# Activation rows stored with their statistics, and a reordered attention and second routing, in a two-layer Macaron block

## The chip, the cores and the metric

The kernel runs on one core of a Trainium2 chip. The metric is the device time of one execution in microseconds (us). The profile gives the span of one profiled execution, which is a little shorter than that execution's own time.

## The reference

Input x has 2 batches of 2048 tokens of width 128. Three layers follow one another: half a feed-forward, an attention, half a feed-forward.

```python
x = x + 0.5 * ffn(layernorm(x))
x = x + attn(layernorm(x))
x = x + 0.5 * ffn(layernorm(x))

# ffn: 4 experts, 128 -> 512 -> 128, each token keeps the one of its largest gate logit
idx = argmax(softmax(x @ Wg + bg))
y = gelu(x @ W1[e] + b1[e]) @ W2[e] + b2[e];  out = y[e == idx]

# attn: linear attention with 32 features
q_prime = elu((x @ Wq.T) @ proj) + 1;  k_prime = elu((x @ Wk.T) @ proj) + 1
kv = k_prime.T @ (x @ Wv.T)
out = (q_prime @ kv) / (sum(q_prime) + 1e-8)
```

Everything is float32.

## The kernel before

**Phases and visits.** A feed-forward of one batch is a phase. `ph` 0 and 1 are the first layer of batches 0 and 1, `ph` 2 and 3 the last layer. The tokens of a batch are sorted by expert into 16 tiles of 128 rows. A phase walks the tiles in 19 visits (16 tiles and 3 for tiles that two experts share). Visit `v` of phase `ph` has the running number `s = 19*ph + v`; there are 76. For a visit TensorE does `up` (line 966: 8 matmuls from `hT_in` and `slab` into `U`) three visits ahead and `down` (line 977: 8 matmuls into `DN`); ScalarE does the gelu between (`hT`, line 1145), VectorE adds the result to the row in `finish` (line 729) and the bias of b2 in `residual` (line 717). In visits 4 to 11 of phases 1 and 2 (`full`) a matmul adds the bias instead. `down(s)` waits for `finish(s-2)`.

**Rows.** The rows lie in HBM as `rows0` and `rows1`, 144 numbers each: 128 activations and 16 columns with mean, reciprocal deviation and token number. GpSimd fetches one sorted tile with an indirect DMA (`gather`, line 430), with a memset of `rest` (line 416) ahead of most of them. VectorE normalises a tile (`norm`, xn, line 705) at the visit that the tables `NORM_*` name; TensorE transposes it (`turn_in`, line 957) in groups, of which tiles 6 and 7 form one that is turned at visit 2. SyncE (SP in the profile) copies the weights of each visit into a `slab`, five visits ahead, and stores the rows: `store_x` (line 306) the activations, `store_stats` (line 287) the 16 columns, each in two halves for each batch, and `store_rows1` after the attention.

**Routing.** `route_hot`, `route_slots`, `route_hots`, `visit_tables` and `route_src` on VectorE, `counts` and `inverse` on TensorE, `place_tiles` on GpSimd and `hots` on ScalarE make the sorted order of the next phase. They lie at visits counted from `hot_at`: HOT0 in phase 0, HOT1 in phases 1 and 2. `route_slots` ends in the tile matrix `A1` (line 651); `route_src` gives the indices `src` (line 691), for which the next gathers wait. `FIRST1 = HOT1 + 4` is the visit at which GpSimd begins to gather the last layer's tiles.

**Attention.** In phase 0 and 1 VectorE takes statistics of finished rows in four groups of tiles; GpSimd raises each to the power -0.5 (`pow_la`, RS, line 401); TensorE projects each group (`side_turn`, `side_kq`) and VectorE scales it (`la_scaled`: lines 750 to 752, LGX, KQ, KM). The last group and all else of the attention of batch 0 lies in visits 0 to 6 of phase 1, that of batch 1 in visits 0 to 6 of phase 2: `la_exp` (ScalarE, which loads another table for it and back), `la_features` (KQ, KR), `la_z`, the sums `la_sum` on TensorE, `la_fold`, `la_gt`, `la_kv`, and four times `lb_num` (TensorE) and `lb_x2` (VectorE), with a power on GpSimd after each (`pow_lb`, line 406). Then `route_hot` follows.

**GpSimd's stream** is written by hand. In phase 1 from visit FIRST1 on it gathers tiles of batch 0 for phase 2 (`gather_first`: one tile and two tiles by turns), and between them runs `pow_la` of batch 1 at visits 10, 12, 15 and 18. In phase 2 it scatters finished tiles of batch 0 to the output (line 442), gathers batch 1's last tiles two at a time, and then scatters all that remain: those of batch 0 from tile `DONE0` on, and 16 of batch 1. Until the pair with tile PAIRS1 of batch 1 every second scatter goes without a `rest` ahead of it, after it all.

**Start.** TensorE fills the time until the first tile with matmuls on `mean_w` (`busy`, line 898); the last such stretch is `busy(24)`, after the gates and the visit tables, and `turn_in` of tile 0 follows it.

## Time and profile before

| | us |
|---|---|
| Three runs | 236.08, 238.13, 237.55 |
| Median | 237.55 |
| The profiled execution, its own time | 237.53 |
| Its span | 235.8 |
| TensorE matmuls busy | 207.2 (88%) |
| VectorE busy | 159.4 (68%) |
| GpSimd busy | 160.2 (68%) |
| ScalarE busy | 126.9 (54%) |

1.73 us of the profiled execution lie outside its span. The busy shares are averages over stages with different limits. PE, DVE, ACT, POOL and SP stand for TensorE, VectorE, ScalarE, GpSimd and SyncE in the rows. In a timeline row the first number is the start in us from the span's start, the second the length in us.

### The profile page before, as it was taken

How to read it: one execution, taken by the hardware profiler on the slowest of the kernel's cores; microseconds unless marked ns; L12 is line 12 of the kernel's file. 1: busy time of each engine (PE TensorE's matmuls, PEld its weight loads, DVE VectorE, ACT ScalarE, POOL GpSimd, SP SyncE). 2: the span in 40 equal slices, each digit the busy share in tenths (PEclk: the TensorE clock that was granted, in tenths of full speed). 3: DMA queues.
4: the chain of work that ended last, by engine and by line, in shares of the span. 5: the costliest groups of instructions: out<-in, count | busy, mean ns of one | idle time of the engine just before them, and what ended most of it. 6: DMA issues, size and time to landing. Idle time of an engine off the chain costs nothing. (4 is left out here: it accounts for less than half of the span.)

```text
span 235.8 us, 6375 instructions
## 1 busy us (share of the span) xinstructions
PE 207.2 (88%) x1786; PEld 195.7 (83%) x1786; DVE 159.4 (68%) x641; ACT 126.9 (54%) x406; POOL 160.2 (68%) x225
## 2 busy tenths in 40 slices
PE   8989996996997999999969998999959899999900
PEld 7879996896997988889969897779959899999900
DVE  3699463579688989698887879788776545553400
ACT  1415055567554586635675676825565567765500
POOL 7221888882728687147138888756878888788775
PEclk9999999998899999999999999999979999999985
DMA  4999259982534462326703852517721976662111
GB/s 103 372 321 254 96 199 351 314 212 83 185 110 167 154 215 69 130 106 237 277 0 116 300 206 83 165 61 281 269 79 42 329 274 222 222 221 103 45 56 45
DMA packets 28454, 41.69 MB, mean 177 GB/s; under 512 B 7795, under 2 KB 14851, under 8 KB 28422
## 3 DMA queue, kind: packets, MB, share of 16 engines
q1 hardware_dynamic: 22368, 34.11, 40.5%
q0 software_dynamic: 3072, 6.82, 11.1%
q10 hardware_dynamic: 2982, 0.36, 1.0%
q8 instruction: 16, 0.26, 0.5%
q14 instruction: 16, 0.13, 0.2%
HBM read 9.41 MB, written 6.82 MB: 69 GB/s over the span
## 5 line engine op out<-in xcount | busy, mean ns | idle before, releaser
L1145 ACT ACTIVATE hT<-U,slab 128x128 f32<-128x128 f32 x304 | 86.7, 370 | 56.4 <-PE U L966 56.3
L966 PE MATMUL U<-hT_in,slab 128*128 (+1 forms) x608 | 82.8, 280 | 1.5 <-ACT hT_in L1139 1.3
L977 PE MATMUL DN<-W,hT 128*128 (+1 forms) x608 | 83.7, 282 | 0.2 <-issue 0.2
L966 PEld LDWEIGHTS U<-hT_in,slab 128*128 128x128 f32 x608 | 74.8, 194 | 2.7 <-issue 2.4
L977 PEld LDWEIGHTS DN<-W,hT 128*128 128x128 f32 x608 | 75.4, 195 | 1.4 <-issue 1.2
L430 POOL DMA_INDIRECT G<-rows,src x64 | 62.5, 977 | 15.2 <-issue 10.2
L729 DVE SCALAR_TENSOR_TENSOR G<-DN,mask,G 128x128 f32 (+1 forms) x76 | 26.4, 348 | 27.3 <-PE DN L977 24.6
L416 POOL MEMSET rest<- 128x512 f32 (+1 forms) x78 | 35.4, 454 | 6.3 <-DVE G L729 0.7
L442 POOL DMA_INDIRECT out_dram<-G x32 | 31.6, 988 | 7.3 <-issue 6.3
L705 DVE TENSOR_SCALAR xn<-G 128x128 f32<-128x128 f32 x64 | 23.7, 389 | 9.3 <-DMA G<-rows,src 9.0
L717 DVE SCALAR_TENSOR_TENSOR G<-slab,mask,G 128x128 f32 (+1 forms) x60 | 21.2, 353 | 6.7 <-DVE G L729 4.0
L1139 ACT ACTIVATE hT_in<-TR 128x128 f32<-128x128 f32 (+1 forms) x44 | 14.4, 327 | 17.8 <-PE TR L957 17.4
L957 PE MATMUL TR<-ident,xn 128*128 128x128 f32 x64 | 14.6, 280 | 7.5 <-DVE xn L705 6.3
L401 POOL TENSOR_TENSOR RS<-VE,neghalf 128x4 f32<-128x4 f32 x8 | 8.5, 1062 | 12.9 <-DVE VE L741 12.8
L406 POOL TENSOR_TENSOR G<-VE,neghalf 128x4 f32<-128x4 f32 x8 | 8.3, 1043 | 12.8 <-DVE VE L799 12.6
L957 PEld LDWEIGHTS TR<-ident,xn 128*128 128x128 f32 x64 | 8.3, 142 | 8.8 <-DVE xn L705 7.2
L898 PE MATMUL DN<-mean_w 128*128 128x128 f32 x104 | 14.6, 300 | 1.1 <-POOL mean_w L362 1.1
L898 PEld LDWEIGHTS DN<-mean_w 128*128 128x128 f32 x104 | 13.9, 215 | 1.1 <-POOL mean_w L362 1.1
L467 POOL TENSOR_TENSOR AV<-A,lane_f 128x256 bf16<-128x256 bf16 x4 | 3.3, 828 | 12.5 <-DVE A L651 6.9
L396 POOL TENSOR_TENSOR MR<-VE,neghalf 128x8 f32<-128x8 f32 x4 | 6.7, 1679 | 5.7 <-DVE VE L564 5.2
L734 DVE BATCH_NORM_STATS2 ST<-G 128x6 f32<-128x128 f32 x32 | 8.8, 287 | 1.6 <-issue 1.4
L656 DVE TENSOR_TENSOR SL<-slot_i,lane_b 128x512 bf16<-128x512 int32 x12 | 8.8, 784 | 0.0
(159 smaller groups left out, 219.7 us busy)
## 6 DMA issues: line engine op xcount, KB each, us to landing
slab<-W SPq DMA_DIRECT2D x76, 322.0 KB, 3.1
rows<-G SPq DMA_DIRECT2D x8, 288.0 KB, 2.1
rows<-X SPq DMA_DIRECT2D x4, 512.0 KB, 9.5
X<-in_L_attn_x_dram SPq DMA_DIRECT2D x4, 256.0 KB, 6.7
X<-in_L_attn_x_dram SPq DMA_DIRECT2D x2, 512.0 KB, 8.8
W<-in_L_ffn_W_dram SPq DMA_DIRECT2D x1, 1024.0 KB, 11.5
W<-in_L_ffn_W_dram SPq DMA_DIRECT2D x4, 256.0 KB, 6.0
G<-rows,src POOLq DMA_INDIRECT x64, 3.2
```

Of the source, the lines that this page charges most:

```text
L416: eng.memset(rest[:, 0:columns], 0.0)
L430: eng.indirect_dma_start(out=row(f, b, t, 0, RW), out_offset=None, in_=(rows0, rows1)[f][b], in_offset=bass.IndirectOffsetOnAxis(ap=src[f] ...
L442: eng.indirect_dma_start(out=out_rows, out_offset=bass.IndirectOffsetOnAxis(ap=index, axis=0), in_=row(1, b, t), in_offset=None, engine_se ...
L705: ffn["norm"].done(eng.tensor_scalar(xn[k % NXN][:, :], row(f, b, t), row(f, b, t, D, 1), row(f, b, t, D + 1, 1), ALU.subtract, ALU.mult))
L717: ffn["res"].done(eng.scalar_tensor_tensor(out=r, in0=slab[s % NSLAB][:, F + NC:SW], scalar=mask[f][b][:, v:v + 1], in1=r, op0=ALU.mult, o ...
L729: ffn["out"].done(eng.scalar_tensor_tensor(out=r, in0=DN[s % 2][:, 0:D], scalar=mask[f][b][:, v:v + 1], in1=r, op0=ALU.mult, op1=ALU.add))
L898: eng.matmul(DN[0][:, 0:P], mean_w[:, :], mean_w[:, :], start=True, stop=True)
L957: last = eng.transpose(TR[:, i * P:(i + 1) * P], xn[k % NXN][:, :], ident[:, :])
L966: i = eng.matmul(U[s % 3][:, c * P:(c + 1) * P], slab[s % NSLAB][:, c * P:(c + 1) * P], hT_in[ph % 2][:, bass.ds(v * P - expert_at[s], P)] ...
L977: i = eng.matmul(DN[s % 2][:, 0:D], hT[s % NHT][:, c * P:(c + 1) * P], W2[:, bass.ds(expert_at[s] + c * NE * D, D)], start=(c == 0 and not ...
L1139: ffn["xTs"].done(eng.activation(hT_in[ph % 2][:, first * P:(first + n) * P], TR[:, 0:n * P], ACT.Copy))
L1145: i = eng.activation(hT[s % NHT][:, c * P:(c + 1) * P], U[s % 3][:, c * P:(c + 1) * P], ACT.Gelu, bias=slab[s % NSLAB][:, F + c:F + c + 1])
```

## The change

**Rows.** Activations and statistics of a batch share one tile `XR` of 144 columns. For batch 1 the load writes straight into it; for batch 0 ScalarE copies the activations over (`copy_rows`, four instructions after the fourth `front_copy`). A half batch is then stored by one DMA of 1152 contiguous numbers for each partition. For batch 0 these two stores stand on SP behind the four loads of W2; for batch 1 at visits 5 and 6 instead of four stores at visits 2, 4, 7 and 8.

**Order of phases 1 and 2, visits 0 to 9.** Each step of the attention comes up to one visit earlier and HOT1 goes from 7 to 6, and with it FIRST1 from 11 to 10. Two instructions of `route_slots` (`end_i`, `flo_i`) move to `visit_tables`.

```diff
@@ -111,9 +111,12 @@
-        X0 = several("X0_", [P, T, D], B)
...
+        XR = several("XR", [P, T, RW], B)
+        X0 = [sb("X0", [P, T, D])[:, :, :], XR[1][:, :, 0:D]]
         ST0 = several("ST0_", [P, T, 6], B)
-        MR0 = several("MR0_", [P, T, RW - D], B)
+        MR0 = [r[:, :, D:RW] for r in XR]
         VE0 = several("VE0_", [P, T], B)
@@ -207,8 +211,8 @@
         NORM_LATE = (-5, -4, -3, -2, -1, 0, 1, 1, 2, 3, 4, 5, 6, 7, 8, 9)
-        NORM_MID = (-5, -4, -3, -2, -1, 0, 0, 1, 1, 2, 2, 3, 4, 5, 7, 8)
-        NORM_EARLY = (-5, -4, -3, -2, -1, 0, 0, 1, 1, 2, 2, 3, 4, 5, 6, 6)
+        NORM_MID = (-5, -4, -3, -2, -1, 0, 0, 0, 3, 3, 4, 4, 5, 5, 7, 8)
+        NORM_EARLY = (-5, -4, -3, -2, -1, 0, 0, 0, 3, 3, 4, 4, 5, 5, 6, 6)
@@ -268,7 +272,7 @@
         UP_LEAD, RES_LEAD, SLAB_LEAD = 3, 2, 5
-        HOT0, HOT1 = 5, 7
+        HOT0, HOT1 = 5, 6
         FIRST0, FIRST1 = HOT0 + 4, HOT1 + 4
@@ -280,11 +284,6 @@
-        def store_stats(eng, b, h):
-            lo, hi = h * T // 2, (h + 1) * T // 2
-            need(eng, ln0["rstd"], 2 * b + h)
-            eng.dma_start(rows0_v[b][:, lo:hi, D:RW], MR0[b][:, lo:hi, :]).then_inc(s_rows0[b], 16)
@@ -300,10 +299,14 @@
-            def store_x(b, h):
-                for i in range(h * XN[b] // 2, (h + 1) * XN[b] // 2):
-                    eng.wait_ge(s_x[b][i], 16)
-                eng.dma_start(rows0_v[b][:, h * H:(h + 1) * H, 0:D], X0[b][:, h * H:(h + 1) * H, :]).then_inc(s_rows0[b], 16)
+            def store_rows0(b, h):
+                need(eng, ln0["rstd"], 2 * b + h)
+                if b == 0:
+                    eng.wait_ge(s_copied, (h + 1) * XN[0] // 2)
+                else:
+                    eng.wait_ge(s_x[b][h], 16)
+                eng.dma_start(rows0_v[b][:, h * H:(h + 1) * H, :].rearrange("p t c -> p (t c)"),
+                              XR[b][:, h * H:(h + 1) * H, :].rearrange("p t c -> p (t c)")).then_inc(s_rows0[b], 16)
@@ -311,10 +314,10 @@
             eng.dma_start(w1_v[:, :, F + NC:SW], b2.unsqueeze(0).to_broadcast([P, NE, D])).then_inc(s_w["b2"], 16)
-            store_x(0, 0)
-            store_x(0, 1)
             for e in range(NE):
                 load_w2(e)
+            store_rows0(0, 0)
+            store_rows0(0, 1)
@@ -349,10 +352,8 @@
                     copy_slab(s + SLAB_LEAD)
-                if ph == 0 and v in (2, 4):
-                    store_x(1, v // 2 - 1)
-                if ph == 0 and v in (7, 8):
-                    store_stats(eng, 1, v - 7)
+                if ph == 0 and v in (5, 6):
+                    store_rows0(1, v - 5)
                 if ph in (1, 2) and 6 <= v < 6 + NG:
@@ -452,12 +453,10 @@
                     pow_la(ph, NG - 1)
-                if ph > 0 and v == 4:
-                    pow_lb(o, 0)
-                if ph == 2 and v == 4:
-                    scatter(0, 0)
-                if ph > 0 and 4 <= v < 3 + NG:
-                    pow_lb(o, v - 3)
+                if ph > 0 and v in (4, 5, 6):
+                    pow_lb(o, v - 4)
+                if ph > 0 and v == 6:
+                    pow_lb(o, 3)
                 if ph < B and v in VAR_AT[ph]:
@@ -476,8 +475,8 @@
-            SCATTERS = {5: (1,), 6: (2,), 7: (3,), 8: (4,), 9: (5,), 10: (6,)}
-            DONE0, PAIRS1 = 7, 10
+            SCATTERS = {v: (v - 4,) for v in range(4, FIRST1)}
+            DONE0, PAIRS1 = FIRST1 - 4, 10
@@ -520,7 +519,7 @@
                     place_tiles(3)
-                if v >= FIRST1:
+                if FIRST1 <= v < FIRST1 + T // 2:
                     gather(1, 1, 2 * (v - FIRST1), columns=2 * P)
@@ -639,10 +638,8 @@
                 need(eng, rt["cb"], ph)
-                did(eng.tensor_tensor(wh3[:, :, :], wh[:, :, :], hot[:, :, :], ALU.mult), False)
-                did(eng.tensor_copy(end_i[:, :], c3[:, 0:NE - 1, T - 1]))
-                did(eng.tensor_reduce(pos[:, :], te(wh3), AX.X, ALU.add), False)
-                did(eng.tensor_scalar(flo_i[:, :], end_i[:, :], 7, None, ALU.arith_shift_right))
+                did(eng.tensor_tensor(wh3[:, :, :], wh[:, :, :], hot[:, :, :], ALU.mult))
+                did(eng.tensor_reduce(pos[:, :], te(wh3), AX.X, ALU.add))
                 did(eng.tensor_copy(pos_i[:, :], pos[:, :]))
@@ -659,6 +656,9 @@
                 e_no = exp_no[:, 1:NE, 0]
+                ends = cum[:, :].rearrange("p (e t) -> p e t", e=NE)[:, 0:NE - 1, T - 1]
+                did(eng.tensor_copy(end_i[:, :], ends))
+                did(eng.tensor_scalar(flo_i[:, :], end_i[:, :], 7, None, ALU.arith_shift_right))
                 did(eng.scalar_tensor_tensor(out=vis[:, :], in0=flo_i[:, :], scalar=float(T - 1), in1=e_no, op0=ALU.min,
@@ -832,22 +832,21 @@
                 f, b = divmod(ph, 2)
+                o = ph - 1
+                if ph in (1, 2) and v == 3:
+                    la_kv(o)
                 finish(s)
                 if ph in (1, 2):
-                    o = ph - 1
                     if v == 1:
-                        la_scaled(o, NG - 1)
+                        la_features(o, 2, NG)
+                        la_z(o, 0, NG)
                     if v == 2:
-                        la_features(o, NG - 1, NG)
-                        la_z(o, NG - 1, NG)
-                    if v == 3:
                         la_gt(o)
-                        la_kv(o)
                     if v == 4:
-                        lb_x2(o, 0)
                         lb_x2(o, 1)
-                    if v in (5, 6):
-                        lb_x2(o, v - 3)
+                    if v == 5:
+                        lb_x2(o, 2)
+                        lb_x2(o, 3)
                 r = (0, 1) if ph == 0 else (1, ph - 1)
@@ -858,6 +857,8 @@
                     norm(*ahead)
+                if ph in (1, 2) and v == 0:
+                    la_scaled(o, NG - 1)
                 if ph == 0 and v == hot_at + 2:
@@ -878,9 +879,9 @@
                     if v == 0:
-                        la_features(o, 0, NG - 1)
-                    if v == 1:
-                        la_z(o, 0, NG - 1)
+                        la_features(o, 0, 2)
+                    if v == 3:
+                        lb_x2(o, 0)
                 if ph < B + 1:
@@ -1016,7 +1017,7 @@
             def la_q(b):
-                need(eng, la["z"], 2 * b + 1)
+                need(eng, la["z"], b)
                 for g in range(NG):
@@ -1072,22 +1073,27 @@
                 ph, v = divmod(s, V)
+                hot_at = HOT0 if ph == 0 else HOT1
+                o = ph - 1
+                if ph in (1, 2) and v == 0:
+                    side_turn(o, NG - 1)
                 down(s)
+                if ph in (1, 2):
+                    if v == 3:
+                        la_kv(o)
+                        la_q(o)
+                    if v == 4:
+                        lb_num(o, 1)
+                    if v == 5:
+                        lb_num(o, 3)
                 for ahead in groups_of(ph, v):
                     turn_in(*ahead)
-                hot_at = HOT0 if ph == 0 else HOT1
                 if ph in (1, 2):
-                    o = ph - 1
                     if v == 0:
-                        side_turn(o, NG - 1)
-                    if v == 1:
                         side_kq(o, NG - 1)
-                    if v == 3:
-                        la_q(o)
-                        la_fold(o)
-                    if v in (4, 5, 6):
-                        lb_num(o, (0, 2, 3)[v - 4])
-                if ph == 0 and v == hot_at + 2:
+                    if v == 2:
+                        la_sum(o, 2, 4)
+                if ph < B + 1 and v == hot_at + 2:
                     counts(ph + 1)
@@ -1103,14 +1109,10 @@
                     if v == 2:
-                        la_sum(o, 2, 4)
-                    if v == 3:
-                        la_kv(o)
-                    if v == 4:
-                        lb_num(o, 1)
-                    if v == hot_at + 2:
-                        counts(ph + 1)
-                    if v == hot_at + (3 if ph == 2 else 4):
+                        la_fold(o)
+                    if v in (3, 4):
+                        lb_num(o, 2 * (v - 3))
+                    if v == hot_at + 4:
                         inverse(ph + 1, 0, NG)
@@ -1133,6 +1135,11 @@
+            def copy_rows(i):
+                lo, hi = i * T // XN[0], (i + 1) * T // XN[0]
+                eng.wait_ge(s_x[0][i], 16)
+                eng.activation(XR[0][:, lo:hi, 0:D], X0[0][:, lo:hi, :], ACT.Copy).then_inc(s_copied, 1)
@@ -1187,10 +1194,10 @@
                 front_copy(k)
+            for i in range(XN[0]):
+                copy_rows(i)
             front_copy(NG)
             front_copy(NG + 1)
-            store_stats(eng, 0, 0)
-            store_stats(eng, 0, 1)
             hots(0, NG - 1)
@@ -1207,16 +1214,16 @@
                 late = ph in (1, 2) and v in (0, 1, 2)
-                if late and v == 1:
-                    la_exp(ph - 1, 3, 4)
-                if late and v > 0:
-                    gelu(s + UP_LEAD - 1)
                 if ph in (1, 2):
...
                         side_copy(o * NG + NG - 1)
+                        la_exp(o, 0, NG)
                     if v == 2:
                         la_part(o)
+                if late and v > 0:
+                    gelu(s + UP_LEAD - 1)
+                if ph in (1, 2):
                     if v == 3:
@@ -1228,8 +1235,6 @@
                         hots(ph + 1, g)
-                if ph < B and v == 18:
-                    la_exp(ph, 0, 3)
```

Two hunks are left out: the new semaphore `s_copied`, and the wait for 32 instead of 64 counts of `s_rows0` ahead of the first gather of a phase.

On SyncE, the program's first DMAs (X, XR: activations; W: W1, then W2 at the line of `load_w2`; rows_0: the HBM rows of batch 0). Before:

```order
L298 DMA X_0<-in_L_attn_x_dram 128x512 x4
L298 DMA X_1<-in_L_attn_x_dram 128x1024 x2
L312 DMA W<-in_L_ffn_W_dram 128x4x512
L313 DMA W<-in_L_ffn_b_dram 128x4x128
L306 DMA rows_0<-X_0 128x8x128 x2
L301 DMA W<-in_L_ffn_W_dram 128x4x128 x4
```

After:

```order
L297 DMA X<-in_L_attn_x_dram 128x512 x4
L297 DMA XR<-in_L_attn_x_dram 128x8x128 x2
L315 DMA W<-in_L_ffn_W_dram 128x4x512
L316 DMA W<-in_L_ffn_b_dram 128x4x128
L300 DMA W<-in_L_ffn_W_dram 128x4x128 x4
L308 DMA rows_0<-XR 128x1152 x2
```

The stores of rows_0 have gone behind W2's loads, and each moves 1152 numbers in a row for each partition.

On GpSimd, from the third `pow_la` of batch 1 (RS1_1) to the fourth, in phase 1 (visits 15 to 18); G1_0 is the last layer's rows of batch 0. Before:

```order
L401 TENSOR_TENSOR RS1_1<-VE1_1,neghalf 128x4
L416 MEMSET rest 128x512
L430 DMA G1_0<-rows1_0,src1_0 128x144
L416 MEMSET rest 128x512
L430 DMA G1_0<-rows1_0,src1_0 128x144
L416 MEMSET rest 128x512
L430 DMA G1_0<-rows1_0,src1_0 128x144
L416 MEMSET rest 128x512
L430 DMA G1_0<-rows1_0,src1_0 128x144
L401 TENSOR_TENSOR RS1_1<-VE1_1,neghalf 128x4
```

After:

```order
L402 TENSOR_TENSOR RS1_1<-VE1_1,neghalf 128x4
L417 MEMSET rest 128x512
L431 DMA G1_0<-rows1_0,src1_0 128x144
L417 MEMSET rest 128x512
L431 DMA G1_0<-rows1_0,src1_0 128x144
L417 MEMSET rest 128x512
L431 DMA G1_0<-rows1_0,src1_0 128x144
L417 MEMSET rest 128x512
L431 DMA G1_0<-rows1_0,src1_0 128x144
L417 MEMSET rest 128x512
L431 DMA G1_0<-rows1_0,src1_0 128x144
L402 TENSOR_TENSOR RS1_1<-VE1_1,neghalf 128x4
```

Four gathers stood between the third and the fourth RS1_1, now five. Between the second and the third it was three and is four; ahead of the second stand three in both.

On VectorE, visits 0 and 1 of phase 2 (KQ1, LGX1, KM1: group 3 of the attention of batch 1; L729 is `finish`, L705 `norm`, L717 `residual`). Before:

```order
L729 SCALAR_TENSOR_TENSOR G1_0<-DN1,mask1_0,G1_0 128x128
L750 COPY LGX1<-S0 128x16
L751 TENSOR_TENSOR KQ1<-S0,RS1_1 128x4x2x32
L752 TENSOR_SCALAR KM1<-KQ1 128x2x128
L705 TENSOR_SCALAR xn7<-G1_0 128x128
L705 TENSOR_SCALAR xn0<-G1_0 128x128
```

After:

```order
L729 SCALAR_TENSOR_TENSOR G1_0<-DN0,mask1_0,G1_0 128x128
L705 TENSOR_SCALAR xn5<-G1_0 128x128
L705 TENSOR_SCALAR xn6<-G1_0 128x128
L705 TENSOR_SCALAR xn7<-G1_0 128x128
L750 COPY LGX1<-S0 128x16
L751 TENSOR_TENSOR KQ1<-S0,RS1_1 128x4x2x32
L752 TENSOR_SCALAR KM1<-KQ1 128x2x128
L717 ISA
L717 SCALAR_TENSOR_TENSOR G1_0<-slab5,mask1_0,G1_0 128x128
L758 SCALAR_TENSOR_TENSOR KQ1<-KQ1,KM1 128x2x128
```

`la_scaled` of the last group stood behind the `finish` of visit 1; now it stands in visit 0, ahead of the `residual` and of all `la_features`.

## Rows read from the trace of the kernel before

**Rows 1.** The chain of work that ended last, its end: start, length, what

```profile
223.57 0.36 DVE G L729
...
225.62 0.96 POOL out_dram L442
...
233.20 0.95 POOL out_dram L442
```

**Rows 2.** Timeline of GpSimd, phases 2 and 3: start, length, what, idle before

```profile
171.56 0.61 POOL L467 TENSOR_TENSOR AV<-A,lane_f 128x256 bf16<-128x256 bf16 x1 [0.60 <-DVE A L651]
...
176.79 0.99 POOL L430 DMA_INDIRECT G<-rows,src  x1 [0.43 <-issue]
...
199.15 0.95 POOL L430 DMA_INDIRECT G<-rows,src  x1 [0.15 <-issue]
...
203.45 0.96 POOL L442 DMA_INDIRECT out_dram<-G  x1 [0.16 <-issue]
...
206.21 0.97 POOL L442 DMA_INDIRECT out_dram<-G  x1 [0.16 <-issue]
```

**Rows 3.** Timeline of all engines, the start of the program

```profile
23.25 5.55 PE L898 MATMUL DN<-mean_w 128*128 128x128 f32 x48
24.10 1.20 POOL L430 DMA_INDIRECT G<-rows,src  x1 [4.30 <-DMA rows<-MR]
...
35.76 0.60 SPq L306 DMA_DIRECT2D rows<-X  x1
...
36.35 0.95 POOL L430 DMA_INDIRECT G<-rows,src  x1 [0.15 <-issue]
...
41.04 0.42 DVE L705 TENSOR_SCALAR xn<-G 128x128 f32<-128x128 f32 x1 [2.48 <-DMA G<-rows,src]
...
41.51 0.44 PE L957 MATMUL TR<-ident,xn 128*128 128x128 f32 x2 [2.25 <-DVE xn L705]
```

**Rows 4.** Busy time in stretches of 2 us; then granted clock, DMA share, GB/s

```profile
8.00:10.00 2.00, 2.00 (x20) 2.00 (x20) 1.90 (x14) 0.79 (x2) 0.26 (x1) 1.00 1.05 407
...
18.00:20.00 2.00, 2.00 (x20) 2.00 (x20) 1.97 (x6) 1.54 (x5) 1.00 (x1) 1.00 1.28 263
```

**Rows 5.** Timeline of GpSimd, phase 1 from visit 10 on

```profile
121.55 1.01 POOL L401 TENSOR_TENSOR RS<-VE,neghalf 128x4 f32<-128x4 f32 x1 [3.39 <-DVE VE L741]
...
123.20 1.04 POOL L430 DMA_INDIRECT G<-rows,src  x1 [0.17 <-issue]
...
127.80 1.05 POOL L401 TENSOR_TENSOR RS<-VE,neghalf 128x4 f32<-128x4 f32 x1
...
139.30 0.96 POOL L430 DMA_INDIRECT G<-rows,src  x1 [0.15 <-issue]
...
141.08 0.96 POOL L430 DMA_INDIRECT G<-rows,src  x1 [0.16 <-issue]
142.06 1.18 POOL L401 TENSOR_TENSOR RS<-VE,neghalf 128x4 f32<-128x4 f32 x1
```

**Rows 6.** Timeline of TensorE, visits 0 and 1 of phase 2

```profile
138.49 1.06 PE L977 MATMUL DN<-W,hT 128*128 x8
...
142.88 1.13 PE L998 MATMUL S<-Wkq,xTs 128*128 128x96 f32 x8
```

**Rows 7.** Timeline of VectorE, phase 2, attention and routing

```profile
144.04 0.17 DVE L750 COPY LGX<-S 128x16 f32<-128x16 f32 x1
...
171.06 0.42 DVE L651 TENSOR_TENSOR A<-tile_i,lane_f 128x256 bf16<-128x256 int32 x1
...
174.85 0.17 DVE L691 TENSOR_SCALAR src<-tok 128x16 int32<-128x16 f32 x1
```

**Rows 8.** Timeline of TensorE around the second routing of phase 2

```profile
172.87 0.25 PE L940 MATMUL S<-AV,SL 128*128 128x32 bf16 x4 [2.22 <-DVE SL L656]
...
174.32 2.07 PE L977 MATMUL DN<-W,hT 128*128 x8
```

**Rows 9.** Busy time in a stretch of 2 us, as in Rows 4

```profile
174.00:176.00 2.00, 2.00 (x17) 1.99 (x18) 1.08 (x5) 1.24 (x5) 1.70 (x3) 0.50 0.09 33
```

3 lines of the change are left out of this document (2 added, 1 removed).

## Prediction

> **What bounds the kernel now.** I read the chain of work that ended last first. The last `finish` ends at 223.93, yet GpSimd goes on scattering until 234.15, one scatter every 1.26 us (225.62 to 233.20 are seven of them) [rows 1]. Those scatters' data were ready before; GpSimd is behind. So the next view is its timeline, to find where it last waited for something [rows 2]. From the first of the last sixteen gathers at 176.79 it is never idle for more than 0.3 us: fifteen steps to 199.15 are 1.49 us each, then come 25 scatters, two in 2.76 us with a `rest` ahead of every second one (203.45 to 206.21). The end is therefore fixed by the start at 176.79, and TensorE's end at 223 has 10 us to spare. That start hangs on the routing: `A1` is done at 171.48, `place_tiles` comes at 171.56, two scatters follow, then the gather [rows 2, 7]. `src`, its other condition, is done at 175.02 [rows 7].
>
> Ahead of that, each step waits in turn for VectorE's chain of attention and routing (phases 1 and 2), and at the start there is one large hole in TensorE: 2.25 us ahead of 41.51, for a tile whose gather was issued at 36.35 and was there only at 41.04 [rows 3].
>
> All times below are on the clock of the trace of before. Its execution took 237.53 us, 0.02 from the median, so a difference in the span is taken as one of the median.
>
> **Start.** The first gather waits for the statistics' stores until 24.10 [rows 3]; without them it could go when `src` is ready. It would go at about 22.9. But TensorE would gain nothing from it there: it is in `busy(24)` from 23.25 to 28.80, and that stretch hangs on the gates and tables, not on the rows [rows 3]. Value: 0. What does count is the hole at 39.3. The gather of tile 7 took 4.7 us from its issue to `norm` (36.35 to 41.04), the first one 2.9 (24.10 to 27.01). Just ahead of it a store of 0.5 MB of activations went out at 35.76 [rows 3]. After the change that store is gone from there and the gather starts 1.2 us sooner: 35.15 plus 2.9 to 3.7 is 38.0 to 38.9, `norm` takes 0.4, and TensorE wants the tile at 39.26. The hole closes, -2.25 us. The stores of batch 1, now at visits 5 and 6 and each waiting for a power of GpSimd, meet the gathers of tiles 11 and 12 and hold the slabs of visits 11 and 12 back; those are wanted some 3 us later. I allow 0.25. **Sum -2.0, bounds -2.25 and 0** (0 if tile 7 is as late as now). The four copies on ScalarE are 0.6 us each like `front_copy` and fall into a stretch in which it waits 3.5 us.
>
> Here a row speaks against the change: batch 1's X now lands in pieces of 512 B. In 8 to 10 us, with the large pieces of X, the queues moved 407 GB/s; in 18 to 20, with rows and W2 in such pieces, 263 [rows 4]. Its first half, 0.5 MB, then takes 0.7 us longer; it was wanted at 13.25 by VectorE and had landed at about 11.5, so nothing waits. The Trainium skill's page "DMA: Bandwidth & Descriptors" (Specifications) says that 512 B and more go at line rate; by that the 0.7 us would be 0. The sum is the same by both.
>
> **Phase 1.** The attention of batch 0 is one chain on VectorE, from `la_scaled` of the last group to `A1`. I laid the instructions out in the new order with their durations. In visits 0 to 5 the chain runs 1 to 3 us ahead of the old one, but TensorE now stands twice (0.8 us in visit 0 for ScalarE's `side_copy`, 1.2 us in visit 5, where `lb_num` of the last group waits for VectorE). `route_hots` (2.3 us) now lies at visit 8 ahead of the `norm` of tile 15, and TensorE wants that tile at visit 10: it stands 1.7 us. `inverse` is done at 119.9 instead of 121.2; `src` at 120.6 instead of 122.4. At visit 12 both orders stand at the same place within 0.5 us. **Value 0, bounds -1.2 and +1.2.** What is left is that GpSimd begins the gathers earlier: 120.7, not 123.20 [rows 5].
>
> **The power that comes late.** This is the step on which the forecast rests. GpSimd then gathers back to back, 1.76 us for one with its `rest` (139.30 to 141.08 are 1.78), with the powers of `pow_la` among them of 1.0 each [rows 5]. The second power ran at 127.80. In the new order `visit_tables` (2.5 us) stands ahead of the variance that it needs, which is then ready at about 127.7: the same time, with the same three gathers ahead. But from there to the fourth power stand nine gathers instead of seven, because they begin a visit earlier. The fourth power was 142.06 to 143.24; two gathers more make it end at 143.24 + 3.5 - 0.1 = 146.6. Before, `la_scaled` took it up at 144.04, in visit 1 [rows 7]. Now `la_scaled` stands in visit 0: TensorE would be ready with `side_kq` at about 141.75 (138.49, plus 0.44 for `side_turn`, 0.9 for `down`, 0.9 for the copy on ScalarE, 0.9 for `side_kq`) instead of 144.01 [rows 6]. So VectorE stands from 141.8 to 146.6, with `residual` and all `la_features` behind it, ScalarE's fourth exp and the gelus behind that, and TensorE's `la_sum` and `down` behind these. The earlier place is worth nothing, and the chain starts 146.6 - 144.04 = 2.55 us later than before.
>
> **Phase 2, from there to the gathers.** From `la_scaled` to `A1` the old chain took 171.48 - 144.04 = 27.4 us [rows 7]; in phase 1 the same instructions took 26.8. Of these, 3.0 are waits for TensorE, so 23.8 are work. The new one has 2.1 us of `la_features` more behind `la_scaled`, and 0.5 less of `norm` and of `end_i`: 25.4, plus 1.1 of waits at `la_kv` and `lb_num`: 26.5. TensorE stands some 4.5 us for KR. After 2.2 us without work at 172.87 it ran a `down` in 2.07 instead of 1.06, at a granted clock of 0.50, its lower level, over 174 to 176 [rows 8, 9]. Some matmuls of the chain fall into such a stretch: +0.6. `A1` = 146.6 + 26.5 + 0.6 = 173.7, against 171.48. `place_tiles` 0.6, two scatters of 1.75, and 0.5 to the gather: 178.3. `src` comes some 3.8 after `A1`, at 177.5, and does not bind. **Sum: 178.3 - 176.79 = +1.5**, bounds -3.9 (the power is not late: `A1` at 168.3, gather at 172.9) and +3.4 (more on the lower clock).
>
> **The tail.** From the first of the last gathers on GpSimd does 16 gathers as before, but 26 scatters instead of 25, since only six go ahead of the gathers. The one more has a `rest` of its own at the end of the row of pairs: 1.26 + 0.2 = **+1.45**. It has no cover, because GpSimd is the bound here.
>
> Total: -2.0 + 0 + 1.5 + 1.45 = +0.95. 237.53 + 0.95 = **238.5 us**.
>
> **Rivals.**
> 1. *The power is in time* (faster). If VectorE gets through visits 10 to 18 of phase 1 early enough, or the gathers begin earlier, nothing holds `la_scaled`. For it speaks that GpSimd was idle 3.39 us ahead of 121.55 [rows 5], so some of this can be used. Against it: nine gathers in a row cannot be shorter than 15.8 us, and the fourth power's variance is ready at 139.7. Then the gather goes at 172.9: -3.9 + 1.45 - 2.0 = -4.45, 233.1 us.
> 2. *The lower clock* (slower). TensorE stands 4.5 us for KR in visits 1 and 2 of phase 2, twice the hole ahead of 172.87. If the lower clock then holds over the next two visits and not a part of one, `la_sum`, `down`, `turn_in` and `up` ahead of `la_fold` double: 2.5 us instead of 0.6. It decides as soon as the hole is the 2.2 us of rows 8 or more at a place with a backlog behind it. 240.4 us.
> 3. *The start gains nothing*: tile 7 is as late as now, because slabs and not the store delay it (its queue was full from 36 to 46 us, and most of that is slabs). 240.5 us.
>
> **How the numbers follow.** The likeliest case has 0.5 (236 to 239.9). Rival 1 has 0.25, rival 2 0.13, rival 3 0.12. The predicted time is that of the first. The range reaches to rival 1 at the one end and over rivals 2 and 3 at the other: 233.0 to 240.8. A measurement of this kernel can tell about 1% from no change, 235.2 and 239.9 here. Faster by over 1%: all of rival 1 and a little of the first, 0.27. Slower: rivals 2 and 3, less their lower parts, 0.22. Same: 0.51.
>
> **What would show it.** In the timeline of after: no hole in TensorE at 39 us while `busy(24)` ends where it did; the fourth RS of phase 1 with five gathers back to back ahead of it and VectorE's LGX of visit 0 in phase 2 with an idle time before it, released by that RS; the gather behind the last routing at 175 to 177 on the new clock; 26 scatters behind the last gather, and no idle time of GpSimd among them. The forecast is wrong if LGX in phase 2 is released by TensorE, or if the hole at 39 us stays.

## The result, and the profile after

The changed kernel takes 244.02 us (median of 4 runs, 242.81 to 244.93); the kernel before, run beside it, 236.81 us (235.76 to 238.13). The ratio is 1.0298, with a 95% interval of 1.0218 to 1.0378: slower by about 7 us. Ratios, here and below, compare undisturbed executions alone, so they can differ a little from the quotient of the medians. The forecast was 238.5 with a range of 233.0 to 240.8. The span of the profiled execution went from 235.8 to 243.2 us, +7.4, and all of this can be placed.

I read the end first, GpSimd's timeline in phases 2 and 3. After:

```profile
177.32 0.62 POOL L466 TENSOR_TENSOR AV<-A,lane_f 128x256 bf16<-128x256 bf16 x1 [1.89 <-DVE A L648]
...
182.56 1.11 POOL L431 DMA_INDIRECT G<-rows,src  x1 [0.43 <-issue]
...
205.07 0.95 POOL L431 DMA_INDIRECT G<-rows,src  x1 [0.15 <-issue]
...
240.59 0.96 POOL L443 DMA_INDIRECT out_dram<-G  x1 [0.30 <-issue]
```

Before, the same three DMAs started at 176.79, 199.15 and 233.20 [rows 1, 2]. So 5.77 us of the loss were there when the last sixteen gathers began, and 240.59 - 182.56 = 58.03 against 56.41 is 1.62 more for the 26th scatter (forecast 1.45). GpSimd is again never idle behind 182.56. The tail is as forecast; the miss lies ahead of it.

The timeline of the start, of all engines (SPq is SyncE issuing DMAs):

```profile
3.77 5.71 SPq L315 DMA_DIRECT2D W<-in_L_ffn_W_dram  x1
...
10.60 6.47 SPq L300 DMA_DIRECT2D W<-in_L_ffn_W_dram  x4
12.16 2.18 ACT L1141 ACTIVATE XR<-X 128x512 f32<-128x512 f32 x4
17.18 1.32 SPq L308 DMA_DIRECT2D rows<-XR  x2
25.58 1.19 POOL L431 DMA_INDIRECT G<-rows,src  x1 [5.89 <-DMA rows<-XR]
30.38 0.33 PE L958 MATMUL TR<-ident,xn 128*128 128x128 f32 x1 [1.69 <-DVE xn L705]
42.24 0.44 PE L958 MATMUL TR<-ident,xn 128*128 128x128 f32 x2 [0.71 <-DVE xn L705]
51.12 0.44 PE L958 MATMUL TR<-ident,xn 128*128 128x128 f32 x2 [0.96 <-DVE xn L705]
```

The first gather was at 24.10 [rows 3] and was to come at 22.9; it came at 25.58, held by the stores of the rows. ScalarE's copies end at 14.34, but SyncE is still issuing W1 and W2 until 17.07, and only then the two stores. TensorE, which is through with `busy(24)` at 28.69, now stands 1.69 us for its first tile. Its hole at tile 7 [rows 3, 2.25 us] has shrunk to 0.71, and a new one of 0.96 stands at 50 us.

GpSimd, VectorE and TensorE around the second power of phase 1 and behind it, in phases 1 and 2:

```profile
127.96 0.20 DVE L682 TENSOR_SCALAR mask<-own 128x20 f32<-128x20 f32 x1
...
129.86 0.17 DVE L741 TENSOR_SCALAR VE<-MV 128x4 f32<-128x4 f32 x1
130.12 1.04 POOL L402 TENSOR_TENSOR RS<-VE,neghalf 128x4 f32<-128x4 f32 x1 [1.96 <-DVE VE L741]
...
146.94 0.96 POOL L431 DMA_INDIRECT G<-rows,src  x1 [0.15 <-issue]
147.92 1.04 POOL L402 TENSOR_TENSOR RS<-VE,neghalf 128x4 f32<-128x4 f32 x1
149.07 0.17 DVE L750 COPY LGX<-S 128x16 f32<-128x16 f32 x1 [3.90 <-POOL RS L402]
151.06 1.00 PE L1010 MATMUL S<-G,KR 128*32 128x128 f32 x16 [2.28 <-DVE KR L762]
...
176.82 0.42 DVE L648 TENSOR_TENSOR A<-tile_i,lane_f 128x256 bf16<-128x256 int32 x1
...
181.18 0.17 DVE L691 TENSOR_SCALAR src<-tok 128x16 int32<-128x16 f32 x1
```

They answer to [rows 5 to 7]. The second power is now *waiting* (1.96 us, for its variance, which stands behind the visit tables that end at 128.16); before it ran at 127.80 without a wait. Nine gathers follow to the fourth, which starts at 147.92 instead of 142.06. `la_scaled` (LGX) stands 3.90 us for it, as the prediction had it, but at 149.07 and not at 144.6.

Behind it TensorE stood 2.28 us. Windows of 2 us there: length; busy time of TensorE, its weight loads, VectorE, ScalarE and GpSimd; then granted clock, DMA share and GB/s. The clock falls to 0.53 in the second one:

```profile
150.00:152.00 2.00, 0.80 (x17) 0.36 (x17) 1.93 (x7) 1.97 (x4) 1.72 (x3) 1.00 0.33 106
152.00:154.00 2.00, 2.00 (x14) 2.00 (x10) 1.90 (x6) 1.01 (x4) 1.73 (x3) 0.53 0.40 132
```

### The profile page after: what moved, and what is told of

The parts are those of the page before. It is cut to its first block, busy times and chain, and to the rows that moved or that the text cites. A ratio compares the mean times of both kernels' runs of the same rounds, so it can differ in the third digit from the quotient of the medians.

```text
span 243.2 us, 6368 instructions
## 1 busy us (share of the span) xinstructions
PE 208.1 (86%) x1786; PEld 195.2 (80%) x1786; DVE 158.2 (65%) x633; ACT 129.6 (53%) x410; POOL 160.2 (66%) x225
## 4 chain that ended last, share of the span: by engine, by line
PE 36%; DVE 13%; POOL 8%; issue 6%; DMA 4%; DVEq 1%; ACT 0%; POOLq 0%
PE DN L978 15%; PE U L967 14%; DMA G<-rows,src 3%; POOL out_dram L443 3%; POOL rest L417 3%; DVE G L793 2%; DVE ST L796 2%; PE TR L958 2%; DVE G L729 2%; PE S L1034 2%; POOL G L431 2%; POOL RS L402 1%; PE S L999 1%; PE S L1010 1%; DVE G L798 1%
## 5 line engine op out<-in xcount | busy, mean ns | idle before, releaser
L978 PE MATMUL DN<-W,hT 128*128 (+1 forms) x608 | 82.3, 279 | 1.1 <-DVE G L729 1.0
L978 PEld LDWEIGHTS DN<-W,hT 128*128 128x128 f32 x608 | 74.5, 193 | 2.0 <-issue 1.9
L967 PEld LDWEIGHTS U<-hT_in,slab 128*128 128x128 f32 x608 | 73.9, 192 | 2.4 <-issue 1.7
L729 DVE SCALAR_TENSOR_TENSOR G<-DN,mask,G 128x128 f32 (+1 forms) x76 | 26.4, 347 | 28.3 <-PE DN L978 24.8
L705 DVE TENSOR_SCALAR xn<-G 128x128 f32<-128x128 f32 x64 | 23.1, 386 | 9.0 <-DMA G<-rows,src 8.9
L717 DVE SCALAR_TENSOR_TENSOR G<-slab,mask,G 128x128 f32 (+1 forms) x60 | 21.1, 351 | 6.6 <-DVE G L729 4.5
L958 PE MATMUL TR<-ident,xn 128*128 128x128 f32 x64 | 15.2, 289 | 9.3 <-DVE xn L705 9.3
L899 PE MATMUL DN<-mean_w 128*128 128x128 f32 x104 | 15.5, 310 | 1.1 <-POOL mean_w L363 1.1
L899 PEld LDWEIGHTS DN<-mean_w 128*128 128x128 f32 x104 | 14.8, 225 | 1.1 <-POOL mean_w L363 1.1
L1034 PE MATMUL S<-KV,QT 128*128 128x512 f32 x16 | 8.8, 630 | 3.0 <-DVE G L793 3.0
L397 POOL TENSOR_TENSOR XR<-VE,neghalf 128x8 f32<-128x8 f32 x4 | 6.8, 1700 | 5.3 <-DVE VE L563 5.3
L999 PE MATMUL S<-Wkq,xTs 128*128 128x96 f32 x64 | 8.5, 276 | 1.7 <-ACT xTs L1161 1.7
```

What stands on the lines that cost most here:

```text
L705: ffn["norm"].done(eng.tensor_scalar(xn[k % NXN][:, :], row(f, b, t), row(f, b, t, D, 1), row(f, b, t, D + 1, 1), ALU.subtract, ALU.mult))
L717: ffn["res"].done(eng.scalar_tensor_tensor(out=r, in0=slab[s % NSLAB][:, F + NC:SW], scalar=mask[f][b][:, v:v + 1], in1=r, op0=ALU.mult, o ...
L729: ffn["out"].done(eng.scalar_tensor_tensor(out=r, in0=DN[s % 2][:, 0:D], scalar=mask[f][b][:, v:v + 1], in1=r, op0=ALU.mult, op1=ALU.add))
L899: eng.matmul(DN[0][:, 0:P], mean_w[:, :], mean_w[:, :], start=True, stop=True)
L958: last = eng.transpose(TR[:, i * P:(i + 1) * P], xn[k % NXN][:, :], ident[:, :])
L967: i = eng.matmul(U[s % 3][:, c * P:(c + 1) * P], slab[s % NSLAB][:, c * P:(c + 1) * P], hT_in[ph % 2][:, bass.ds(v * P - expert_at[s], P)] ...
```

## The experiments

The record numbers the chips of these runs (8, 9, 4 and 11, in the order in which they ran), but not the chip of the traces so far. On all four the kernel before takes 248 to 251 us, so a ratio is read against it on the same chip, and instants up to the last gathers are compared between traces. Up to those gathers they agree: the kernel before has them at 176.79 and, on chip 4, at 176.31. The instants, in us from the span's start; the last column is the stretch from the last power of phase 0 to the last gathers, which leaves the start out:

| kernel | first gather | last power of phase 0 | second, fourth power of phase 1 | wait of LGX in phase 2 | first of the last 16 gathers | stretch |
|---|---|---|---|---|---|---|
| before | 24.10 | 86.50 | 127.80, 142.06 | 0 | 176.79 | 90.3 |
| before_again | 24.00 | 86.03 | 127.31, 141.58 | 0 | 176.31 | 90.3 |
| after | 25.58 | 87.03 | 130.12, 147.92 | 3.90 | 182.56 | 95.5 |
| after_again | 25.36 | 86.25 | 129.37, 147.19 | 3.90 | 181.52 | 95.3 |
| rows_only | 25.33 | 85.78 | 127.06, 141.34 | 0 | 176.05 | 90.3 |
| order_only | 23.28 | 84.73 | 127.84, 145.62 | 3.89 | 178.98 | 94.3 |
| powers_first | 25.47 | 86.72 | 129.83, 144.05 | 1.12 | 177.35 | 90.6 |
| stores_first | 23.02 | 84.03 | 127.18, 145.03 | 3.96 | 178.40 | 94.4 |
| tables_late | 25.52 | 86.20 | 127.42, 145.27 | 3.54 | 179.93 | 93.7 |
| first_late | 25.75 | 86.36 | 129.58, 143.82 | 1.11 | 178.97 | 92.6 |
| rows_first | 22.60 | 83.37 | 124.65, 138.93 | 0 | 173.68 | 90.3 |
| mended | 22.77 | 83.30 | 124.53, 139.96 | 1.11 | 173.75 | 90.5 |
| mended_again | 22.69 | 83.67 | 124.83, 140.28 | 1.12 | 173.61 | 89.9 |
| rows_first_again | 22.65 | 83.28 | 124.57, 138.83 | 0 | 173.56 | 90.3 |
| rows_spaced | 23.60 | 84.48 | 125.77, 140.04 | 0 | 174.87 | 90.4 |
| mended_spaced | 23.07 | 83.72 | 124.93, 140.37 | 1.12 | 173.78 | 90.1 |

**The halves.** `rows_only` is the kernel before with XR, `copy_rows` and `store_rows0`; `order_only` has the rest of the diff. In short, rows_only against the kernel before:

```diff
-            store_x(0, 0)
-            store_x(0, 1)
             for e in range(NE):
                 load_w2(e)
+            store_rows0(0, 0)
+            store_rows0(0, 1)
```

and of order_only one line (its other ones are those of the change in phases 1 and 2):

```diff
-        HOT0, HOT1 = 5, 7
+        HOT0, HOT1 = 5, 6
```

> Only the first half of the change: rows and statistics in one tile, stored by one DMA per half behind W2; attention, routing and GpSimd's stream as before. Theory 1 (the order of phases 1 and 2 costs the time): the start loses about 1 us and a later stretch bound by VectorE takes half of it back, 237 to 238 us. Theory 2 (the stores cost it, through a late first gather): 241 us or more.

> Only the second half: the changed order of visits 0 to 9 and HOT1 6, with the rows stored as before. Theory 1: VectorE's LGX of visit 0 in phase 2 waits some 4 us for the fourth RS of phase 1, the last gathers begin some 5 us later than before, 242 to 244 us. Theory 2: 237 to 239 us.

Measured (before 249.99): rows_only 251.79, ratio 1.012 (1.0027 to 1.0214); order_only 256.37, ratio 1.0267 (1.0184 to 1.0351). The order carries most of the loss, and the wait of 3.89 us of LGX is in it alone. The last column says the same without the start: 90.3 in the old order, 94.3 in order_only, so 4.0 us; the 1.0 to 1.3 more in after and after_again is the lower clock (below). The rows' half holds the first gather until 25.33, by the same stores. Its last gathers come no later than before, though; where its 1.2% arises, if the lower end of the interval is not the truth, the traces don't show.

**The order's wait.** `powers_first` is the changed kernel with the power of visits 15 and 18 ahead of the gathers of the visit before:

```diff
-                if v >= FIRST1:
+                if v in (15, 18):
+                    gather_first(1, 0, s, v - 1 - FIRST1)
+                if v >= FIRST1 and v not in (14, 17):
                     gather_first(1, 0, s, v - FIRST1)
```

> The changed kernel, in which GpSimd's gathers of visits 14 and 17 of phase 1 stand behind the powers of visits 15 and 18 and not ahead of them; three and four gathers lie between the powers as before the change. Theory 1 (two gathers more ahead of the fourth power hold la_scaled): the fourth RS ends at about 145.4 instead of 148.96 and the whole behind it comes 3.5 us earlier, 240 to 241 us. Rival (the chain on VectorE itself has become longer, the power is only the last of several late things): under 1 us gained, 243 to 244 us.

Measured: 254.23, ratio 1.0211 (1.0124 to 1.0298); beside the 1.0298 of after that is no clear gain in time, so the instants have to tell. The timeline of GpSimd, third and fourth power:

```profile
136.08 1.05 POOL L402 TENSOR_TENSOR RS<-VE,neghalf 128x4 f32<-128x4 f32 x1
...
144.05 1.04 POOL L402 TENSOR_TENSOR RS<-VE,neghalf 128x4 f32<-128x4 f32 x1
```

Seven gathers between second and fourth again; the fourth comes 3.1 to 3.9 us sooner than in after_again and after, and the last gathers 4.2 to 5.2 sooner, of which 1.0 to 1.3 is the lower clock that this execution did not have. That the power is late because it stands behind nine gathers is shown. `first_late` gets the same in another way:

```diff
-        FIRST0, FIRST1 = HOT0 + 4, HOT1 + 4
+        FIRST0, FIRST1 = HOT0 + 4, HOT1 + 5
```

> The changed kernel, but the gathers of phases 1 and 2 begin at visit 11, as in the kernel before, instead of visit 10. Theory A (the power is late because two gathers more stand ahead of it): four gathers between the third power and the fourth, the fourth ends at 145 to 146 instead of 148.96, la_scaled in visit 0 of phase 2 waits 1 us or less for it, the tail has 25 scatters; the first of the last gathers comes 3 to 4 us earlier than in the changed kernel, ratio to the kernel before 1.005 to 1.015. Theory B (the new order of VectorE and TensorE itself is slower from la_scaled on): la_scaled's wait is taken by another wait of the same length, and the ratio stays above 1.02.

Measured (before 250.99): 253.14, ratio 1.0113 (1.0074 to 1.0152). The fourth power is at 143.82 and LGX waits 1.11, as theory A has it, and no other wait of that length took its place. The last gathers come 2.6 to 3.6 us sooner than in after_again and after; three scatters stand ahead of them now, not two, which are taken from the tail. `tables_late` tests the second power alone:

```diff
-                    if v == hot_at + 5:
+                    if v == hot_at + (6 if ph == 1 else 5):
                         visit_tables(*r)
```

> The changed kernel with one edit: in phase 1 the visit tables of the next phase stand at visit 12 instead of 11, so behind the second variance on VectorE and not ahead of it. Theory A (they are what makes the second power late, and the fourth, behind nine gathers, with it): the second power follows the first without a wait for its variance, 1.9 to 2 us earlier than in the changed kernel, the fourth too; la_scaled in visit 0 of phase 2 waits 2 us instead of 3.9, and the first of the last gathers comes 1.5 to 2 us earlier. Theory B (the fourth power is set by its own variance or by the finish that the gathers wait for): the fourth power moves by under 0.5 us.

Measured (before 251.39): 257.65, ratio 1.0304 (1.0194 to 1.0415). GpSimd in this kernel, first and second power:

```profile
122.92 1.04 POOL L402 TENSOR_TENSOR RS<-VE,neghalf 128x4 f32<-128x4 f32 x1 [0.38 <-DVE VE L741]
127.42 1.06 POOL L402 TENSOR_TENSOR RS<-VE,neghalf 128x4 f32<-128x4 f32 x1
```

The wait of 1.96 is gone, and second and fourth power come 1.95 and 1.92 us sooner than in after_again: theory A. LGX of phase 2 still waits 3.54, not 2, since VectorE, which the third power no longer holds for 2.46 us, reaches it sooner as well; the last gathers come 1.6 us sooner. The gain isn't seen in the time: on these chips an earlier start of the last stage was mostly lost (below).

**The start.** `stores_first` is the changed kernel with the two stores ahead of the loop of `load_w2`; `rows_first` is rows_only with the same edit.

```diff
+            store_rows0(0, 0)
+            store_rows0(0, 1)
             for e in range(NE):
                 load_w2(e)
-            store_rows0(0, 0)
-            store_rows0(0, 1)
```

> The changed kernel with the two stores of batch 0's rows ahead of the four loads of W2. If their place behind W2 makes the first gather late (25.58 instead of 24.10), it goes at about 23, when src is ready, the 1.7 us hole of TensorE ahead of 30.38 closes, and 1 to 2 us are gained, 242 to 243 us. If the 512 B pieces of batch 1's X, which stand ahead of both, are the cause, the gather stays at 25 or later and nothing is gained.

> The kernel before with the rows' half of the change alone, but with the two stores of batch 0 ahead of the four loads of W2. Theory A (the stores' place behind W2 is what spoils the start): the first gather goes when its indices are ready, near 22.9 instead of 25.3, phase 0's powers come 1.5 to 3 us earlier than in the kernel before, the hole of TensorE at 39 us is under 0.8 us; that gives 1 to 2 us in the end, ratio 0.992 to 0.997. Theory B (the hole is due to slabs, the rows' stores do not matter): the hole stays at 1.5 us or more and the ratio is within 0.3% of 1.

Measured: stores_first (before 249.99) 255.98, ratio 1.0206 (1.0065 to 1.0347), an interval too wide for a gain of 1 to 2 us; rows_first (before 250.99) 250.11, ratio 0.994 (0.9893 to 0.9987), on chip 4 (rows_first_again, before 251.39) 249.89, 0.9988 (0.993 to 1.0047). In rows_first, GpSimd's first gather and TensorE at tiles 6 and 7:

```profile
22.60 1.20 POOL L431 DMA_INDIRECT G<-rows,src  x1 [3.01 <-DVE src L692]
...
38.97 0.44 PE L958 MATMUL TR<-ident,xn 128*128 128x128 f32 x2
```

The gather now waits for its indices and no longer for a store, TensorE has no hole at 39 us, and the last gathers come at 173.68, 2.6 to 3.1 us ahead of the kernel before. The term of the start is -2.5 to -3 and not -2, if the stores do not stand behind W2; with them there it is nothing or a small loss. A part of it may be luck of the execution: order_only, whose start is that of the kernel before, had its first gather at 23.28 and no hole at tile 7, and ended phase 0 1.3 to 1.8 us ahead of the kernel before.

**All mends.** `mended` is the changed kernel with the edits of stores_first, powers_first and tables_late; `after_again` is the changed kernel beside it.

> The changed kernel once more, unchanged, so that the other runs of this call have it beside them. If the slowdown is the order's and does not depend on the chip, the ratio to the kernel before is 1.02 to 1.035 again, la_scaled of the last group waits 3.9 us for the fourth power in visit 0 of phase 2, and the first of the last sixteen gathers comes 5 to 6 us later than in the kernel before. If much of it was the longer last stage of one execution, the ratio is under 1.015.

> The changed kernel with three mends: the two stores of batch 0's rows ahead of the loads of W2; in phase 1 the visit tables of the next phase at visit 12 instead of 11, behind the second variance; and the powers of visits 15 and 18 each ahead of the gathers of the visit before. Theory A (these are the three causes of the loss before the last stage): first gather near 23.0, second power of phase 1 near 127, fourth near 141, la_scaled in visit 0 of phase 2 waits for nothing of GpSimd, the first of the last sixteen gathers 6 to 9 us earlier than in the changed kernel and 1 to 3 earlier than in the kernel before; one scatter more in the tail costs 1.5, so the ratio is 0.992 to 1.0. Theory B (an earlier la_scaled only moves the wait to KR or to lb_num): the first of the last gathers no more than 4 us earlier than in the changed kernel, ratio 1.01 or more.

Measured: after_again 258.16 (six executions, 254.14 to 260.10) against 250.99 of the kernel before; the record has no ratio with an interval for it. mended 251.02, ratio 1.0001 (0.9962 to 1.004): 7 us under the median of after_again, but only 3 under its quickest execution. Up to the last gathers theory A holds (173.75, forecast 1 to 3 ahead of the kernel before, measured 2.6 to 3.0), though LGX still waits 1.11 us for the power, where no wait was expected. But that is where rows_first stands in the old order (173.68). The new order, freed of its waits, has gained nothing on the old one, and has one scatter more behind it. And the 3 us do not reach the end.

**Where they go.** In the first two traces 34.05 and 35.52 us lie between the last of these gathers and the last scatter; in all others up to here 46.0 to 51.3. Was this the kernels, or where they ran?

> The kernel before once more, for its trace beside the others of this call. If the long last stage of the runs so far (48 to 51 us from the last of the last gathers to the last scatter, 34.05 in the first trace of the kernel before) belongs to the chip and not to the changes, this run shows it too on that chip, with TensorE and not GpSimd as the engine that ends last; if it belongs to the changes, this run shows 34 us. Ratio 1.0 within 0.5%.

Measured: 251.27, ratio 1.0044 (0.9981 to 1.0106), and 198.61 to 246.49, 47.9 us. It is not the changes. Whether it is the chip itself or something else of the first group of runs the record can't tell. Windows of 10 us of before_again, with the columns as above:

```profile
190.00:200.00 10.00, 7.52 (x43) 6.80 (x44) 1.74 (x6) 3.32 (x12) 8.60 (x14) 0.77 0.43 134
200.00:210.00 10.00, 4.59 (x28) 3.86 (x26) 1.90 (x6) 2.35 (x9) 8.03 (x11) 0.84 0.27 94
```

and the same ones of the first trace of the kernel before:

```profile
190.00:200.00 10.00, 10.00 (x92) 10.00 (x91) 4.99 (x16) 7.08 (x27) 8.57 (x14) 1.00 0.72 243
200.00:210.00 10.00, 10.00 (x92) 10.00 (x92) 4.84 (x16) 7.17 (x26) 8.14 (x12) 1.00 0.62 216
```

GpSimd issues its gathers at the same pace in both, but on chip 4 TensorE does 71 instructions where it did 184, with the DMA engines less busy than before. The granted clock (0.77 and 0.84) is too little lower to account for that. The waits of before_again, 176 to 216 us, do not name the cause:

```profile
DVE G L729 <- remote: 16.4, 4, 7.1
ACT hT L1145 <- PE U L966: 15.3, 6, 4.1
SPq L19 <- DVE G L717: 15.8, 6, 4.0
```

`remote` is a release that the profile ties to no instruction of the core. The last line is SyncE's: its slab copies wait for VectorE's `residual`, and not the other way round. So late slabs, the reason that the expectations below assume, are not what holds TensorE. The copy that SyncE issued at 190.10, for a visit five ahead, had its last packet through at 192.72, and TensorE is at the `up` that reads it only after 210. The copies issued at 186.36, 194.47 and 198.25 are in time by some 20 us as well. What does hold TensorE is open.

Afterwards TensorE ends the run together with GpSimd, and a stage that starts earlier ends only a little earlier.

> The kernel with the three mends once more, next to a trace of the kernel before of the same chip. Up to the first of the last sixteen gathers it should be 3 us ahead of the kernel before (173.75 against 176.79 in the traces so far). Theory A (where GpSimd ends last, this comes out, less 1.5 us for the 26th scatter): ratio 0.991 to 0.997 if the last stage is as in the first trace. Theory B (where TensorE waits for slabs in the last stage, an earlier start of it is lost there): ratio 0.997 to 1.004.

> The rows' half of the change in the old order, with the stores ahead of W2, once more, next to a trace of the kernel before of the same chip. It should be 3 us ahead of the kernel before at the first of the last gathers, and it has 25 scatters in the tail and not 26. Theory A (GpSimd ends last): ratio 0.985 to 0.99. Theory B (TensorE waits for slabs in the last stage): 0.99 to 0.998, as in the call before (0.994).

Measured: mended_again 251.12, ratio 1.002 (0.9959 to 1.0082); rows_first_again 0.9988. The first is theory B's number, the second lies just above it: the 3 us are lost. That they are lost to slabs, as theory B has it, is not borne out.

**Spread gathers.** Do the sixteen gathers in a row hold TensorE back? (The expectations put it down to the slabs.) `rows_spaced` is rows_first, `mended_spaced` is mended, each with

```diff
                 s = 2 * V + v
-                if v < FIRST1:
-                    begun(s)
+                begun(s)
```

so that GpSimd gathers two tiles for each visit of phase 2.

> The rows' half of the change in the old order with the stores ahead of W2 (3 us ahead of the kernel before at the first of the last gathers), and one edit: from visit 11 of phase 2 on GpSimd waits for the finish of the visit before and then gathers two tiles, instead of gathering all sixteen in a row; the 25 scatters come behind as before. Theory A (the sixteen gathers in a row hold the slabs back, and TensorE with them, on the chips of the last three calls): TensorE's 8 or so us without work between 185 and 215 shrink to under 3, and the last scatter comes at 238 or sooner instead of 242 to 247, ratio 0.96 to 0.98 there; on a chip like that of the first traces GpSimd is the bound, and the ratio is 0.99 to 1.01. Theory B (the slabs come late there for another reason): TensorE's holes stay, and GpSimd's scatters start later on top of it, ratio 0.995 or more.

> The kernel with the three mends in the changed order and the same edit in phase 2, from visit 10 on. Up to the first of the last gathers it stands where the rows' half in the old order stands (173.6 to 173.75), so the new order has by then gained nothing over the old one; with one scatter more behind the gathers it should be 1.3 to 1.5 us behind it if GpSimd ends last, and level with it if TensorE does. Theory A (gathers in a row hold the slabs back): ratio 0.965 to 0.985 on the chips of the last three calls. Theory B: 1.0 or more.

Measured (before 248.37): rows_spaced 245.12, ratio 0.9866 (0.9822 to 0.9909); mended_spaced 245.35, ratio 0.9888 (0.9837 to 0.9939). Both beat the kernel before, by less than theory A said. Windows of rows_spaced:

```profile
180.00:190.00 10.00, 9.10 (x80) 8.73 (x79) 5.54 (x20) 6.30 (x23) 7.95 (x13) 1.00 0.80 273
190.00:200.00 10.00, 8.27 (x60) 7.89 (x60) 3.39 (x11) 4.96 (x19) 7.95 (x13) 0.86 0.56 186
200.00:210.00 10.00, 6.66 (x55) 6.28 (x53) 2.48 (x8) 3.00 (x11) 8.21 (x12) 0.97 0.40 143
210.00:220.00 10.00, 4.97 (x24) 4.58 (x25) 2.22 (x8) 2.56 (x9) 6.78 (x11) 0.72 0.20 72
```

TensorE does 60 instructions in 190 to 200, and 70 in mended_spaced; in the twelve traces on chips 8, 9 and 4, all with the gathers in a row, it does 33 to 51. From the first of the last gathers to the last scatter it is 66.6 us in both spaced kernels, against 68.8 to 73.0 in rows_first and mended and their repeats. So gathers in a row do hold TensorE back there, though not by the slabs; but the hole moves to 200 to 220, where the scatters now run in a row. That these act in the same way is what the windows suggest; it was not tried. No kernel without the spacing was traced on chip 11, so what the spacing alone is worth has to be taken across chips: 0.7 to 1.2% for rows_spaced (rows_first had 0.994 and 0.9988), 1.1 to 1.3% for mended_spaced (mended had 1.0001 and 1.002). How the two kernels do where GpSimd is the bound, as in the first traces, was not measured. By more than 1%, no other kernel of the study was faster than the kernel before.

## Why the prediction was wrong

The mechanism on which it rested was right: LGX in visit 0 of phase 2 is released by the fourth power, behind nine gathers. The steps that failed are the start, the time at which the second power is ready, and two sizes behind the fourth power; they add to the miss. Forecast for the last gathers was 176.3 (178.3 - 2.0); measured 182.56; 6.3 us to place, and 0.2 of the tail.

- **Start, forecast -2.0, measured +0.5 (2.5 of the miss).** "The first gather could go when `src` is ready": it went at 25.58, because I gave the stores no price for their place. The diff puts them behind W2's loads, and I looked only at the time at which ScalarE's copies are done. The second half of that step, that `busy(24)` pins TensorE, holds for an earlier first gather only: with the later one TensorE stood 1.69 us ahead of 30.38. In rows_first and stores_first, with the gather at 22.60 and 23.02, neither this hole nor the one at tile 7 is there, and phase 0 ends 3.1 and 2.5 us earlier than in the kernel before (last power 86.50). The stores take about as long to land in both (5.6 us, 5.1 in stores_first); what mattered is that they were issued at 17.18 and not at 12.80, as in stores_first.
- **The second power, "127.80, the same time", measured 130.12 (1.8 more, beyond the 2.5).** I took its variance to be ready at 127.7, just in time, and so at no cost. It was ready at 130.03, which is 129.5 without the 0.5 of the start, behind the visit tables. tables_late takes this away and gets 1.9 us back. An instant that I had laid out myself, with no slack at all, had no bound for coming late.
- **From the power to `A1`, forecast 27.1, measured 28.3 (1.2).** From the start of LGX to the end of `A1` it is 28.2 here and in tables_late, 27.9 in after_again, and 26.9 in order_only, powers_first, stores_first, first_late and mended. In the three longer ones two windows of 2 us between 150 and 156 us show a clock of 0.53 to 0.62; in the other five it is 1.00 throughout. So the work was right (26.5 forecast, 26.9 measured), and rival 2 happened in part in that execution: 1.0 to 1.3 us instead of 0.6. The hole ahead of it was 2.3 us long and not 4.5.
- **`A1` to the gather, forecast 4.6, measured 5.3 (0.7).** It was 5.3 in the kernel before as well, 171.48 to 176.79 [rows 2, 7]. The two scatters take 3.9 and not 3.5 (the first is 1.42 long), and the memset with its gap ahead of the gather 0.7 and not 0.5.
- **Phase 1, forecast 0 within -1.2 and +1.2.** `src` is at 121.74 instead of 122.19 though phase 0 ended 0.5 later: -1.0. It is worth nothing, as the prediction said, because what follows waits for the powers.
- **Tail, forecast +1.45, measured +1.6.** Right: one scatter fewer has its place ahead of the last gathers, where GpSimd waits anyway, and one more stands where it is the bound.

2.5 + 1.8 + 1.2 + 0.7 + 0.2 is 6.4, against 7.4 - 0.95 = 6.45. The first two are one after the other in the same chain, so both count in full. Of the rivals, the one that says that the start gains nothing was right in its sign. Its reason is only half answered: tile 7's gather was issued 1.35 us later than before (37.70), which is the stores' doing, but it also took 4.1 us to `norm` with batch 1's store gone from there, where 2.9 to 3.7 was forecast and 4.7 measured before. In order_only that store still went out at 35.48, and the gather took 3.8. So the store was a small part of those 4.7 us. Had rivals 2 and 3 been taken together, the sum would have been 240.5 + 1.9 = 242.4, still outside the range and 1.6 too low. The range had no case in which two of these come together.

The paragraph on pieces of 512 B forecast that batch 1's X lands 0.7 us later. It took 9.5 us from issue to landing instead of 8.8 (median of its two DMAs), and nothing waited for it. The window of 8 to 10 us, with X in pieces of 512 B, moves 338 GB/s where before moved 407 [rows 4]. The rule of the Trainium skill's page "DMA: Bandwidth & Descriptors" (Specifications), that 512 B and more go at line rate, would have changed nothing. The two windows of 8 to 10 us do not agree with it. The 263 GB/s that the prediction took for such pieces were a wrong reading: 1324 of the packets that start in 18 to 20 us of before are pieces of 64 B, of the statistics' stores, and 830 of 512 B. The same window of after, with the stores of 1152 numbers in a row, moves 353. None of this is in the sum, since what counts is when the stores are issued. A small slip, on which nothing rests: the terms given for 141.75 add up to 141.63.

## What to carry to other kernels

When a DMA moves to another place in an engine's stream, price the issue of everything that now stands ahead of it, not only its own size: a store that was meant to be faster let the first gather go 1.5 us later. When work with fixed length (here gathers) is begun earlier but shares an engine with short steps on which another engine's chain hangs, count how many of it stand ahead of each short step, and move those steps forward with it. And a forecast that needs two engines to meet without slack should carry a term for the one that is late.
